# Token rows kept in the convolution's plane order from the first load to the last store, and row statistics taken four groups ahead, in a one-core feed-forward, convolution and attention block

## The reference

```
x = x + 0.5 * ffn(layernorm(x))
x = x + attention(layernorm(x))
x = x + 0.5 * ffn(layernorm(x))

ffn(x):        routing = softmax(x @ gate_w.T)                  # 8 experts
               x * (routing @ in_scale) @ sign(weight).T * (routing @ out_scale) + bias
attention(x):  x = conv1d(x, width 3, 1024 -> 768) + conv_b;  q, k, v = split(x)   # 256 each
               blocks of 128 tokens, 16 heads of 64, causal mask inside a block,
               softmax, @ v, @ wo, @ proj_w + proj_b
```

## Time and profile before

| | |
|---|---|
| time, three runs | 1061.52, 1066.28, 1067.0 us; median 1066.28 us |
| the profiled execution's own time | 1063.77 us |
| its span, first to last instruction | 1062.0 us |
| TensorE busy | 928.4 us (87%) |
| VectorE busy | 715.6 us (67%) |
| ScalarE busy | 453.2 us (43%) |
| GpSimd busy | 370.4 us (35%) |
| moved by DMA | 119.88 MB, 113 GB/s on average |

### The profile page before, as it was taken

One profiled execution on the slowest core, in us unless ns is written; L12 is line 12 of the kernel. 1 busy time (PEld: TensorE's weight loads), 2 busy tenths in 40 slices (PEclk: granted clock), 3 DMA queues, 4 the chain that ended last, 5 costly groups with the idle time before them and its releaser, 6 DMA issues.

```text
span 1062.0 us, 15599 instructions
## 1 busy us (share of the span) xinstructions
PE 928.4 (87%) x4960; PEld 701.2 (66%) x4960; DVE 715.6 (67%) x1469; ACT 453.2 (43%) x1127; POOL 370.4 (35%) x307
## 2 busy tenths in 40 slices
PE   3898889886999899897987997899798888999997
PEld 2576667663334687686766886778577666688786
DVE  5677775567898888455487288368729946766652
ACT  3434444342134236144565356345625554334331
POOL 2145555564443210000121233214213441455555
PEclk8799999997999999998997999999999999999999
DMA  9333322321324341753002022211141264343233
GB/s 298 129 120 119 119 79 79 139 80 70 117 91 149 119 149 50 286 205 148 26 2 93 7 81 70 70 39 59 59 130 61 96 254 169 116 160 139 94 129 114
DMA packets 41469, 119.88 MB, mean 113 GB/s; under 512 B 5696, under 2 KB 14912, under 8 KB 40000
## 3 DMA queue, kind: packets, MB, share of 16 engines
q1 hardware_dynamic: 41408, 119.11, 32.3%
HBM read 87.64 MB, written 31.46 MB: 112 GB/s over the span
## 4 chain that ended last, share of the span: by engine, by line
PE 48%; DVE 15%; issue 5%; ACT 4%; DMA 2%; SPq 0%; POOL 0%; DVEq 0%; POOLq 0%; ACTq 0%
PE a_p_g L1762 16%; PE a_p_g L624 11%; PE c_p_m L1219 5%; PE c_p_m L1221 3%; PE c_p_m L1223 3%; PE c_p_m L1222 3%; PE a_p_s L1786 2%; ACT a_s L1559 2%; DVE a_sums L1663 2%; DVE a_s L1660 2%; PE a_p_o L1810 1%; DVE a_pt L1677 1%; DMA c_raw<-in_conv_w_dram 1%; DVE c_xs_lo L1625 1%; PE a_p_s L567 1%
## 5 line engine op out<-in xcount | busy, mean ns | idle before, releaser
L1492 POOL TENSOR_TENSOR a_s<-a_s,a_sums 128x512 f32<-128x512 f32 x64 | 66.6, 1040 | 309.1 <-DVE a_sums L1669 309.1
L276 POOL TENSOR_TENSOR f_y<-f_y,f_res 128x512 f32<-128x512 f32 x64 | 82.8, 1294 | 144.8 <-DVE f_y L478 144.5
L1559 ACT ACTIVATE a_s<-a_s,a_nmx 128x128 f32<-128x128 f32 x256 | 99.3, 390 | 44.5 <-DVE a_nmx L1665 44.5
L1762 PE MATMUL a_p_g<-c_xs_hi,x_room 128*128 128x512 f32 x256 | 97.7, 429 | 20.5 <-DVE c_xs_lo L1625 12.2
L624 PE MATMUL f_p_m<-f_wsign,f_a_hi 128*128 128x512 f32 x256 | 106.3, 415 | 0.0
L624 PE MATMUL f_p_m<-f_wsign,f_a_lo 128*128 128x512 f32 x256 | 102.6, 401 | 0.0
L624 PE MATMUL a_p_g<-f_wsign,f_a_hi 128*128 128x512 f32 x256 | 102.5, 400 | 0.0
L624 PE MATMUL a_p_g<-f_wsign,f_a_lo 128*128 128x512 f32 x256 | 100.4, 392 | 0.0
L1219 PE MATMUL c_p_m<-c_vf,c_ring_f 128*128 128x512 f32 x192 | 87.0, 610 | 9.3 <-DVE c_ring_f L896 6.2
L1221 PE MATMUL c_p_m<-c_vh,c_ring 128*128 128x512 f32 x192 | 76.3, 397 | 9.9 <-DVE c_ring L1102 8.1
L273 POOL TENSOR_TENSOR f_res<-f_res,f_hbias 128x512 f32<-128x512 f32 x64 | 83.2, 1300 | 0.0
(11 more groups left out here) (218 smaller groups left out, 2240.3 us busy)
## 6 DMA issues: line engine op xcount, KB each, us to landing
c_raw<-in_conv_w_dram SPq DMA_DIRECT2D x24, 768.0 KB, 4.3
f_w_raw<-in_w_t_dram SPq DMA_DIRECT2D x8, 1024.0 KB, 11.0
f_res<-in_x_dram SPq DMA_DIRECT2D x16, 512.0 KB, 4.0
x_after_ffn<-f_y SPq DMA_DIRECT2D x8, 1024.0 KB, 6.1
f_xin<-x_after_attention SPq DMA_DIRECT2D x8, 1024.0 KB, 7.2
f_res<-x_after_attention SPq DMA_DIRECT2D x16, 512.0 KB, 3.9
out_dram<-f_y SPq DMA_DIRECT2D x8, 1024.0 KB, 6.1
f_xin<-in_x_dram SPq DMA_DIRECT2D x7, 1024.0 KB, 8.2
```

Of the source, the lines that this page charges most:

```text
L276: pool.tensor_tensor(y[:, p, t, h], y[:, p, t, h], res[:, t, h], ALU.add).then_inc(y_done, 1)
L1492: pool.tensor_tensor(s[:, r], s[:, r], sums[:, r].unsqueeze(2).broadcast_to([P, 4, P]), ALU.mult).then_inc(probs_ready, 1)
L1559: done = act.activation(s[:, r, h, :], s[:, r, h, :], ACT.Exp, bias=nmx[:, r, h:h + 1], scale=SCALE, accum_out=sums[:, r, h:h + 1])
L1762: mm = pe.matmul(p_g[:, bank, :], a, b, start=n == 0, stop=n == len(pairs) - 1)
```

## The change

Rows are brought into plane order when they are first loaded: partition 32s+m of a tile holds token 4m+s. The first feed-forward loads x and the residual rows from the input so, keeps them so, and stores them so; attention and the second feed-forward work on rows in that order; the last store puts them back. Then `copy_normed`, `first_split_high`, `first_split_low`, `split_high` and `split_low` copy runs of 32 neighbouring elements instead of steps over four planes. The mask is built for the new order, in twelve GpSimd instructions that run after the convolution's, where there were two. The loads of x in the first feed-forward and the stores of the second become two transfers for each group instead of one. Apart from that, `stats` runs four groups ahead, at the end of quarter 3, ahead of the y multiply; `load_x` runs four groups ahead too; and the hardware loop over groups is written out.

```diff
 def group_loop(eng, body):
-    body(0, 0)
-    with eng.Fori(0, (NG - 4) // 2) as i:
-        body(2 * i + 1, 1)
-        body(2 * i + 2, 0)
-    for g in range(NG - 3, NG):
+    for g in range(NG):
         body(g, g % 2)
...
+    src_planes = src.rearrange("(g t m s) d -> g t s m d", t=FT, s=4, m=P // 4)
+    dst_planes = dst.rearrange("(g t m s) d -> g t s m d", t=FT, s=4, m=P // 4)
...
         def load_x(g, p):
-            if isinstance(g, int) and g == 2:
-                sp.wait_ge(t_full, 4)
-            sp.dma_start(xin[:, p], srcv[g]).then_inc(x_loaded[p], 16)
+            if isinstance(g, int) and g in (2, 3):
+                sp.wait_ge(t_full, 4 * g - 4)
+            if turn:
+                sp.dma_start(xin[:, p], srcv[g]).then_inc(x_loaded[p], 16)
+            else:
+                for t in range(FT):
+                    sp.dma_start(xin[:, p, t, :], src_planes[g, t]).then_inc(x_loaded[p], 16)
...
-            sp.dma_start(res[:, t, :], srcv[g][:, t, :]).then_inc(res_loaded[t], 16)
+            sp.dma_start(res[:, t, :], srcv[g][:, t, :] if turn else src_planes[g, t]).then_inc(res_loaded[t], 16)
...
         def store(g, p):
-            sp.wait_ge(y_done, 4 * g + 4)
-            sp.dma_start(dstv[g], y[:, p]).then_inc(y_stored[p], 16)
+            if turn:
+                for t in range(FT):
+                    sp.wait_ge(y_done, 4 * g + 2 * t + 2)
+                    sp.dma_start(dst_planes[g, t], y[:, p, t, :]).then_inc(y_stored[p], 16)
+            else:
+                sp.wait_ge(y_done, 4 * g + 4)
+                sp.dma_start(dstv[g], y[:, p]).then_inc(y_stored[p], 16)
...
-            if exists(g + 3):
-                sp.wait_ge(t_full, 4 * g + 8)
-                load_x(g + 3, 1 - p)
+            if exists(g + 4):
+                sp.wait_ge(t_full, 4 * g + 12)
+                load_x(g + 4, p)
...
                 f.load_res(0, t)
+                f.load_x(3, 1)
...
-                if q == 0 and exists(g + 3):
-                    stats(g + 3, 1 - p)
...
                 if q == 3 and exists(g + 1):
                     low(g + 1, 1 - p, KD - 1)
+                if q == 3 and exists(g + 4):
+                    stats(g + 4, p)
...
                 f.softmax(1)
+                f.stats(3, 1)
...
-            act.copy(Xp[:, k0:k0 + 4, :, quads].rearrange("p k s m -> p k m s"),
-                     bank[:].rearrange("p (k m s) -> p k m s", k=4, s=4)).then_inc(n_copied, 1)
+            act.copy(Xp[:, k0:k0 + 4, :, quads], bank[:].rearrange("p (k s m) -> p k s m", k=4, s=4)).then_inc(n_copied, 1)
...
-                act.copy(xs[0][:, c, :].rearrange("p (m s) -> p m s", s=4), tokens(c)).then_inc(xs_hi, 1)
+                act.copy(xs[0][:, c, :].rearrange("p (t s m) -> p t s m", t=GT, s=4), tokens(c)).then_inc(xs_hi, 1)
...
-                high, low = (x[:, c, :].rearrange("p (m s) -> p m s", s=4) for x in xs)
+                high, low = (x[:, c, :].rearrange("p (t s m) -> p t s m", t=GT, s=4) for x in xs)
```

More of the change, by code:

```diff
@@ L221, in stored @@
         def stored():
-            sp.wait_ge(y_stored[0], 16 * (NG // 2) + 1)
-            sp.wait_ge(y_stored[1], 16 * (NG // 2) + 1)
+            for count in y_stored:
+                sp.wait_ge(count, 16 * (NG // 2) * (FT if turn else 1) + 1)
         return SyncSteps(load_x, load_tiles, load_gate, load_scales, load_w, load_bias, load_res, store, stored, body)
@@ L476, in body @@
                     else:
-                        wait(dve, y_stored[p], 8 * (g - p) + 1)
+                        wait(dve, y_stored[p], 16 * (g - p) + 1)
                 dve.tensor_tensor(y[:, p, q // 2, q % 2 * HALF:q % 2 * HALF + HALF], p_m[:, q % 2, :],
@@ L814, with by_tile @@
 UNITS_C = STAGES * NCH
+def by_tile(planes):
+    return planes.rearrange("p s (t m) -> p t s m", t=GT)
 class Convolution:
@@ L856, in first_split_high @@
         act.wait_ge(self.y_final, c + 1)
-        tokens = self.Y[:, c, :, 0:GTOK // 4].rearrange("p s m -> p m s")
-        act.copy(self.xs[0][:, c, :].rearrange("p (m s) -> p m s", s=4), tokens).then_inc(self.xs_hi, 1)
+        tokens = by_tile(self.Y[:, c, :, 0:GTOK // 4])
+        act.copy(self.xs[0][:, c, :].rearrange("p (t s m) -> p t s m", t=GT, s=4), tokens).then_inc(self.xs_hi, 1)
     def first_split_low(self, dve, c):
-        high, low = (x[:, c, :].rearrange("p (m s) -> p m s", s=4) for x in self.xs)
-        tokens = self.Y[:, c, :, 0:GTOK // 4].rearrange("p s m -> p m s")
+        high, low = (x[:, c, :].rearrange("p (t s m) -> p t s m", t=GT, s=4) for x in self.xs)
+        tokens = by_tile(self.Y[:, c, :, 0:GTOK // 4])
         dve.wait_ge(self.xs_hi, c + 1)
@@ L1342, in attention_phase @@
         mask = sb("mask", [P, P], small + 128)
+        order = conv.room[:, 2, 0:P]
         p_s, p_t, p_g = ps("p_s", [P, 2, HALF]), ps("p_t", [P, 2, HALF]), ps("p_g", [P, 2, HALF])
@@ L1457, in _ @@
                 s2.load_res(0, t)
+            s2.load_x(3, 1)
             for t in range(GT):
@@ L1469, in _ @@
             s2 = second.pool(pool)
-            pool.memset(mask[:], 0.0).then_inc(mask_made, 1)
-            pool.wait_ge(mask_made, 1)
-            pool.affine_select(out=mask[:], in_=mask[:], compare_op=ALU.is_ge, fill=MASKED, base=0,
-                               pattern=[[-1, P]], channel_multiplier=1).then_inc(mask_made, 1)
+            pool.wait_ge(conv.first_taken, NCH)
+            for a in range(4):
+                rows = slice(32 * a, 32 * a + 32)
+                wait(pool, mask_made, 3 * a)
+                pool.memset(order[:], 0.0).then_inc(mask_made, 1)
+                pool.wait_ge(mask_made, 3 * a + 1)
+                pool.affine_select(out=order[:].rearrange("p (s m) -> p s m", s=4), in_=order[:].rearrange("p (s m) -> p s m", s=4),
+                                   compare_op=ALU.is_ge, fill=MASKED, base=-(P - 1) * a,
+                                   pattern=[[-1, 4], [-4, P // 4]], channel_multiplier=4).then_inc(mask_made, 1)
+                pool.wait_ge(mask_made, 3 * a + 2)
+                pool.tensor_copy(mask[rows, :], order[rows, :]).then_inc(mask_made, 1)
             pool.wait_ge(proj_loaded, 2 * 16)
@@ L1719, in _ @@
             s2.softmax(1)
+            s2.stats(3, 1)
             group_loop(dve, s2.body)
```

10 lines of the change are left out of this document (5 added, 5 removed).

## The result

The changed kernel took 1116.76 us as median of four runs (1116.32 to 1118.81), the kernel before 1066.64 us; the ratio is 1.048, with a 95% interval of 1.044 to 1.052. The prediction was 1078 us in a range of 1058 to 1097. The direction was right, and so was the cause that was named, plane transfers on four DMA engines. The price was not: the loss is 50 us where 12 were forecast.

The account below looks back on a forecast made before the run. TensorE, busy 87% of the span, was taken as the bound. From 1063.8 us: +26.5 start, -9.5 and -0.5 copies, -1.8 convolution, -6.5 attention, +3.7 end = 1075.7; as median 1078, range 1058 to 1097.

Parts of the forecast that it names:

- The number of engines: Loads of x and residual rows and output stores in four planes run on four DMA engines at 25.6 GB/s each.
- The start: Up to the first `low` of group 1: plane loads on four engines make the stage 26.5 us late.
- Bodies 1 to 3: First feed-forward: 23.0 us of four-engine transfers fit a group of about 25.5; late residual rows take back 0.75 us a passage.
- the four engines become the bound: Rival for bodies 1 to 3: at 15% less rate, three groups each 4 us longer, start 5; about 1092; chance 0.2.
- The copies: First feed-forward: copies at contiguous pace end TensorE's waits 1.36 us sooner a body, 9.5 us over bodies 1 to 7.
- The convolution: At its end, five `split_low` on the chain take 3.2 us instead of 5.01, a gain of 1.8 us.
- Attention: Six VectorE copies a group for three groups save up to 0.49 us each, 8.8 us; 6.5 were taken.
- The statistics: First feed-forward: `stats` ahead of the y multiply gains 3.0 us if GpSimd is not late; counted as 0.
- costs and gives nothing: Second feed-forward: the moved `stats` has no effect, since TensorE's 20.3 busy us of 20.7 hide it.
- The final stores: At the end, the stores of groups 6 and 7 on four engines land 3.7 us later.

Follow-up runs that it names:

- token-order transfers: The changed kernel with x, residual rows and last stores moved by the old pattern of 128 rows, only its time being valid: 1036.85 us, 0.974 of the kernel before.
- two runs: The changed kernel with the first feed-forward's store of y issued ahead of the loads: 1108.21 us; with store, then residual rows, then x: 1112.80 us.
- the last run: The changed kernel with the start's plane loads and the bodies' x loads cut into pieces of 32 rows, residual rows of groups 1 to 7 whole: 1067.62 us.
- the order alone: The kernel before with only `stats` and `load_x` four groups ahead and the loop over groups written out: 1058.20 us, 0.995 of the kernel before.

## Why the prediction was wrong, step by step

**The number of engines: right**, with its rate, 25.6 GB/s for each forecast, 26.2 measured.

**The start: mechanism right, size short.** Forecast were 26.5 us; measured are 31.9 at the first `low` of group 1 (80.8 against 48.9) and 34.9 at the end of group 0. The first transfers came about when they should: the first tile's statistics began at 10.58 us (9.6 forecast), and TensorE, which had waited for the gate, began its logits at 28.9, where the sum has gate and scales landed by 29.9 (28.1 and 1.8). X of group 1 took longer, 28.6 instead of 24.9. The term that failed first is the one behind: the bias was there at 38.7 instead of 36.4, and x of group 2 at 51.4 instead of 46.6. The sum puts the next two weight pieces (5.2 us) behind x of group 2. But SyncE was in their issues from 27.59 to 37.1 us, and from 38 to 44 us DMA moved 231 to 248 GB/s with a share of 1.02 to 1.04, more than the four engines' 105: they went beside x of group 2, and with them the sum would have it landed at 51.8. Then the statistics: the program takes those of both tiles when the whole group has landed, so `scale` follows 2.9 us behind it (54.31 less 51.41) and not 1.8. X of group 3 was there at 76.6 instead of 72.2; what of this is which transfer was not taken apart. While the four engines worked off x, SyncE itself stood in its issues, as its timeline shows:

```profile
6.31 5.69 SPq L185 DMA_DIRECT2D f_gateT<-in_gate_t_dram  x1
12.05 9.90 SPq L192 DMA_DIRECT2D f_res<-in_ics_dram  x1
```

An issue takes 0.3 to 0.5 us when nothing stands before it (the earlier trace rows for one). Of the last 3.0 us, 1.8 are the moved statistics: between the last two y adds of group 0 are 7.08 us, before 5.26, because `stats` now stands ahead of the last y multiply. The other 1.2 were not taken apart; TensorE's granted clock was 0.50 from 30 to 40 us and from 45 to 60, behind stretches in which it idled.

**Bodies 1 to 3: this is the step that failed.** The text has "23.0 us of the four engines in a group of about 25.5: just under a new bound", and follows the residual rows alone to the next y add. The 23.0 us of data were right: the four engines moved them from about 99 to 123 us. What was missed is who waits at their end. The sum was compared with the length of a group, as if the transfers could spread over it. They can't. X is released by TensorE's last transposes, which end only 2 to 3.5 us ahead of the last y add (SyncE gets to it at 97.3, 134.6 and 171.7 us; the y adds end at 100.8, 136.6 and 173.7), and the residual tiles and the store stand behind it. So all of it begins close to the last y add, the store has the whole queue before it, and its consumer, `out_normalise`, is due after 12.8 us. VectorE waits 10.3 to 11.5 us in each of the three bodies and TensorE 31.7 us in all; with 4.3 us more of TensorE's busy time at the lower clock (73.6 against 69.3) and less the gains of copies and order, this is the 29.0 us. With token-order transfers, where these waits are missing, the three groups take 74.8 us for 110.3. Putting another transfer last moves the wait and does not remove it (two runs, which also hold the residual rows back); a shorter queue does shorten it (the last run). The rival "the four engines become the bound" lay nearest with 1092, but for a wrong reason: four engines busy for 23.0 us in a group of 36.8 are not full. Its number does not follow either: 23.0 us at 15% less rate are 27.1, so 1.6 us a group over 25.5 and not 4, and 1078 with 12 and 5 would be 1095. In groups 4 to 7, without a load of x, the queue is 10.2 us shorter and the loss is gone but for 3.1 us (94.6 against 91.5 with token order).

**The copies: pace right, worth 7.0 us for 9.5.** `copy_normed` took 606 ns for 595, `first_split_low` 687 for 640. With token-order transfers groups 1 to 7 took 14.3 us less than before, 7.0 of it beyond what the order alone gives (7.3); 9.5 were forecast for these copies. The convolution gave 1.8, the term; in the other profiles with the new copies from the table it gave 1.5 to 3.6.

**Attention: 10.4 us for 6.5.** The ScalarE copies had no price in the sum. Putting them back costs 4 to 6 us, so they are a term that was missing. The sum also took all of a copy's gain from waits, while part of the measured one is TensorE's own busy time (311.3 us in the stage for 313.5 before).

**The statistics: 0 in the sum, 3.0 if GpSimd is not late.** With sixteen engines the order alone gave 4.2 us in the first feed-forward: 7.3 in groups 1 to 7, less 3.1 in the start. Of these 3.1, 1.8 are the statistics ahead of the last y multiply of group 0, which move the end of that group and so this cut. The other 1.3 stand already at the first `low` of group 1 (50.1 for 48.9); in that execution the statistics of group 1 began 2.2 us later (13.90 for 11.74), in a part of the program that did not change. That time lies between 11.2 and 13.9 us in the profiles with token-order transfers, so these 1.3 need not be the change's. None of this was in the sum. On four engines the gain was covered by the waits for the store. In the second feed-forward "costs and gives nothing" was off by 1.7, of which 0.9 lie ahead of its first group's end (68.5 us from the cut for 69.4) and 0.8 behind it.

**The final stores: 6.2 us for 3.7.** The form was right. GpSimd's timeline has the last y add, and the stretch after it shows four engines at 105 GB/s:

```profile
1102.53 1.26 POOL L283 TENSOR_TENSOR f_y<-f_y,f_res 128x512 f32<-128x512 f32 x1 [1.32 <-DVE f_y L485]
```

```profile
1105.00:1110.00 5.00, 0.00 (x0) 0.00 (x0) 0.00 (x0) 0.00 (x0) 0.00 (x0) 0.55 0.25 105
```

From 1103.8 to the span's end are 10.7 us where 8.2 were forecast (1057.5 to 1065.7). The sum lets the four engines run at the full rate from the first of these stores on; four stretches of 2 us from 1088 to 1096 show 57, 244, 61 and 86 GB/s, where a residual tile was still on its way beside them (244 GB/s are more than four engines moved anywhere).

**The sum again.** It gave 1075.7 us for the profiled run, which took 1116.7. The differences, measured less forecast: start +8.4 (34.9 for 26.5); groups 1 to 3 +33.1 (+29.0 for the -4.1 of their three bodies' copies); groups 4 to 7 +1.2 (-4.7 for -5.9); convolution 0; attention -3.9; second feed-forward -0.7; end +2.5; what lies outside the span +0.4. Together 41.0. Three quarters (31.7 us of TensorE's waits) are one wait that the text did not name.

## What to carry to other kernels

When a transfer's pattern is rearranged, look first at its outermost dimension: with four planes outermost it had a quarter of the engines, and cutting it into four transfers of 32 rows brought 72 us back. Compare a queue of transfers with the moment when the last one's consumer is due, counted from the event that releases them, and not with the length of the iteration: here 23.2 us against 12.8; a buffer that is overwritten in place makes its store such a transfer. And follow every transfer of a queue to its consumer: here all were issued within 5 us, and two other orders only chose which of them was late. A transfer whose issue waits for a late event also holds back all that stand behind it in the program.

## What the hardware did that I had not expected

- SyncE stood in an issue for 5.69 and then 9.90 us while four engines worked off 512 KB loads; the small gate load, of another shape, was there 22.5 us after its issue began, where it took 9.0 before.
- Pieces of 32 rows on sixteen busy engines moved 245 GB/s in a stretch where whole tiles moved 314.
- The kernel in which two engines carried each plane load took 1238 us, 121 more than with four.
- Of 18 `split_low` in attention most took 684 ns and some 1176, in the same loop and with the same shape.
